# Attention and routed FFN layer: order of the first loads, and the turning and splitting of the first x by halves

## The reference

```python
k = x @ W_lat + b_lat                                # (2, 512, 128), keys and values of all heads
q = (x @ W_d + b_d).reshape(Bx, Tx, NH, L)           # 16 heads of 128
att = jnp.einsum('bhtl,bsl->bhts', q, k) * scale     # causal mask, softmax
y = jnp.einsum('bhts,bsl->bhtl', att, k)
return y @ W_proj + b_proj                           # then layer norm, FFN on 256 of 512 rows, layer norm
```

## Time and profile before

| what | before |
|---|---|
| time, median of 3 runs | 280.67 us (280.57 to 280.73) |
| the profiled execution's own time | 280.85 us |
| its span, first to last instruction | 279.1 us |
| TensorE busy | 271.7 us (97%) |
| VectorE, ScalarE, GpSimd busy | 218.8, 212.3, 154.2 us |

### The profile page before, as it was taken

How to read it: one execution, slowest core, us unless ns; L and a number is a source line. 1 busy time by engine, 2 the same in 40 slices (tenths; PEclk the granted TensorE clock), 3 DMA queues, 4 the chain that set the end, 5 groups by cost and what they waited for, 6 DMA issues and landing times.

```text
span 279.1 us, 6206 instructions
## 1 busy us (share of the span) xinstructions
PE 271.7 (97%) x1885; PEld 247.0 (89%) x1885; DVE 218.8 (78%) x701; ACT 212.3 (76%) x578; POOL 154.2 (55%) x214
## 2 busy tenths in 40 slices
PE   8999999999999999999999999999999999999991
PEld 4878999999999998999999999999999999999990
DVE  2698777777777777788789888899988887779882
ACT  3689877777787778887787877787777778879471
POOL 5458444444433336555666866665657847238652
PEclk9999999999999999999999999999999999999997
DMA  5594110111101111111111111110112200020151
GB/s 178 144 293 124 39 40 28 30 36 38 34 25 35 38 39 38 40 38 42 38 38 40 38 40 38 39 37 22 38 39 79 78 21 21 1 76 2 58 171 38
DMA packets 18842, 15.53 MB, mean 56 GB/s; under 512 B 1641, under 2 KB 18178, under 8 KB 18818
## 3 DMA queue, kind: packets, MB, share of 16 engines
q1 hardware_dynamic: 18242, 13.65, 16.4%
q0 software_dynamic: 576, 1.58, 1.6%
HBM read 12.60 MB, written 2.63 MB: 55 GB/s over the span
## 4 chain that ended last, share of the span: by engine, by line
PE 97%; DVE 0%; POOLq 0%; issue 0%; ACT 0%; DVEq 0%
PE bank L412 21%; PE bank L414 20%; PE bank L413 20%; PE bank L547 9%; PE ps_out L412 7%; PE ps_out L413 6%; PE ps_out L414 6%; PE bank L527 3%; PE bank L637 3%; PE bank L470 1%; PE bank L424 1%; POOLq L60 0%; PE bank L676 0%; PE bank L678 0%; PE bank L557 0%
## 5 line engine op out<-in xcount | busy, mean ns | idle before, releaser
L841 ACT ACTIVATE probs<-probs,negmax 128x512 f32<-128x512 f32 (+3 forms) x128 | 72.6, 575 | 6.0 <-DVE negmax L1026 4.6
L1384 POOL TENSOR_TENSOR wd_hi<-wd_raw,zero 128x256 fp32r<-128x256 f32 x31 | 23.8, 768 | 87.5 <-DVE probs L1098 84.5
L849 ACT CAST pT_hi<-bank 128x512 fp32r<-128x512 f32 (+2 forms) x96 | 43.4, 488 | 27.7 <-PE bank L547 27.3
L1026 DVE CUSTOM_DVE_ANT_0 probs<-bank,mask_row 128x512 f32<-128x512 f32 (+3 forms) x128 | 59.2, 482 | 0.7 <-PE bank L504 0.7
L1035 DVE TENSOR_TENSOR pT_lo<-bank,pT_hi 128x512 fp32r<-128x512 f32 (+2 forms) x96 | 52.8, 552 | 6.0 <-ACT pT_hi L849 5.6
L547 PEld LDWEIGHTS bank<-ident_r,prob_words 128*128 128x128 f32 x310 | 33.0, 140 | 5.5 <-ACT probs L893 0.4
L412 PE MATMUL ps_out<-wp_hi,yT_hi 128*128 128x256 f32 x124 | 37.0, 299 | 0.0
L412 PE MATMUL bank<-kT_hi,qT_hi 128*128 128x256 f32 (+2 forms) x94 | 36.5, 388 | 0.0
L413 PE MATMUL ps_out<-wp_lo,yT_hi 128*128 128x256 f32 x124 | 35.0, 282 | 0.0
L414 PE MATMUL ps_out<-wp_hi,yT_lo 128*128 128x256 f32 x124 | 34.9, 282 | 0.0
L1055 DVE TENSOR_TENSOR yT_lo<-bank,yT_hi 128x512 fp32r<-128x512 f32 x31 | 21.4, 690 | 15.9 <-PE bank L414 14.1
(11 more groups left out here) (203 smaller groups left out, 732.1 us busy)
## 6 DMA issues: line engine op xcount, KB each, us to landing
wd_raw<-in_L_attn_W_d SPq DMA_DIRECT2D x32, 128.0 KB, 2.2
wp_raw<-in_L_attn_W_proj SPq DMA_DIRECT2D x32, 128.0 KB, 2.1
wf_raw<-in_L_ffn_w SPq DMA_DIRECT2D x2, 1024.0 KB, 6.7
x_nat<-in_L_attn_x SPq DMA_DIRECT2D x4, 256.0 KB, 3.4
out<-z_all SPq DMA_DIRECT2D x4, 256.0 KB, 2.3
picked<-ranked SPq DMA_DIRECT2D x2, 258.0 KB, 2.7
wlat_raw<-in_L_attn_W_lat SPq DMA_DIRECT2D x1, 128.0 KB, 3.8
bproj_all<-in_L_attn_b_proj SPq DMA_DIRECT2D x1, 128.0 KB, 3.4
```

Of the source, the lines that this page charges most:

```text
L841: act.activation(p_tile(s, j), p_tile(s, j), ACT.Exp, bias=negmax[:, s, j:j + 1], scale=-1.0, accum_out=sums[:, s, j:j + 1]).then_inc(exp_ ...
L849: act.copy(pT_hi[:, dst], src).then_inc(pt_hi_done, 1)
L1026: dve.tensor_tensor_reduce(p_tile(s, j), score_bank[j], mask_row[:, (TILES - 1 - j) * P:], -SCALE, -MASKED, ALU.add, ALU.min, accum_out=ne ...
L1384: pool.tensor_tensor(hi, src, nothing, ALU.add).then_inc(hi_done, 1)
```

## The change

1. **Loads.** SyncE issues x half 0, W_lat, x half 1 in place of x half 0, x half 1, W_lat.
2. **Turning.** The first x is turned into four half banks: half 0 into `ps_t0[:, 0:256]` and `ps_t1[:, 0:256]`, half 1 into `ps_s2[:, 0:256]` and `ps_s10[:, 0:256]`. Every pair of transposes signals `x_turned` (four signals; before, two, both from the second half).
3. **Splitting.** ScalarE makes four copies of 128x256 in place of two of 128x512; VectorE four subtractions of 128x256 in place of two of 128x512. The counts of `x_turned`, `x_hi_done` and `x_split` for the second x move up by two.
4. **Idle matmuls.** One (512 columns) after the turning of half 0 (`BETWEEN`), and one after half 1 (`AWAKE`); before, two after half 1.
5. **The key projection.** The same six products in another order: hi·hi and lo·hi of c = 0, hi·hi and lo·hi of c = 1, hi·lo of c = 0, the bias, hi·lo of c = 1. The first one waits for three of four copies of x.
6. **The bias** is turned into `ps_s3`, since `ps_s2` now holds a half of x.

```diff
@@ -253,6 +253,11 @@
             _, _, src, dst = turns[n]
             return (ps_s3[:, P:3 * P] if n == 2 and at.fixed == UNITS else src), dst
+        x_banks = [[ps_t0[:, 0:KEEP], ps_t1[:, 0:KEEP]], [ps_s2[:, 0:KEEP], ps_s10[:, 0:KEEP]]]
+
+        def x_half(t, half, c):
+            return t[:, c, half * KEEP:(half + 1) * KEEP]
+
         def yT_of(at):
             return (last_yT_hi, last_yT_lo) if at.fixed == UNITS + 1 else (yT_hi, yT_lo)
@@ -295,7 +300,7 @@
                             body(Period(i * 2 + q, q, i))
                 p = first + 2 * times
-        WAKING, AWAKE = 6, 2
+        WAKING, BETWEEN, AWAKE = 6, (4,), (4,)
         CONSTS = 7
 
@@ -351,13 +356,14 @@
                 wait(sp, wp_split, unit - 1)
                 sp.dma_start(wp_raw[place][:], W_proj[bass.ds(head * LAT, LAT), :]).then_inc(wp_in[place], 16)
-            def load_x(b):
-                for j in range(0, TILES, 2):
+            def load_x(b, halves=range(2)):
+                for j in (half * 2 for half in halves):
                     sp.dma_start(x_nat[:, b * TILES + j:b * TILES + j + 2, :],
                                  x[b, j * P:(j + 2) * P].rearrange("(j p) d -> p j d", p=P)).then_inc(x_in[b][j // 2], 16)
-            load_x(0)
+            load_x(0, (0,))
             sp.dma_start(wlat_raw[:], W_lat.rearrange("(c p) l -> p c l", p=P)).then_inc(wlat_in, 16)
+            load_x(0, (1,))
             load_wd(0, 0, 0)
             sp.dma_start(bias_rows[0:HEADS, :], b_d.rearrange("(h l) -> h l", l=LAT)).then_inc(bias_in, 16)
             sp.dma_start(bias_rows[B_LAT:B_LAT + 1, :], b_lat.rearrange("(a l) -> a l", a=1)).then_inc(bias_in, 16)
@@ -417,39 +423,43 @@
                 for half in range(2):
                     pe.wait_ge(x_in[b][half], 16)
                     for c in range(CH):
-                        dst = (ps_t0, ps_t1)[c]
+                        dst = (ps_t0, ps_t1)[c][:, half * KEEP:(half + 1) * KEEP] if b else x_banks[half][c]
                         if b and half == 0:
                             pe.wait_ge(x_split, c + 1)
-                        for j in range(2 * half, 2 * half + 2):
+                        for j in range(2):
                             last = pe.transpose(dst[:, j * P:(j + 1) * P].bitcast(F32R),
-                                                x_words[:, b * TILES + j, c * P:(c + 1) * P], ident_r[:, :])
-                        if half:
+                                                x_words[:, b * TILES + 2 * half + j, c * P:(c + 1) * P], ident_r[:, :])
+                        if half or not b:
                             last.then_inc(x_turned, 1)
+                    if not b and half == 0:
+                        keep_awake(BETWEEN)
             def project_k_first():
                 w_hi, w_lo, x_hi, x_lo = wlat_hi, wlat_lo, xT_hi[0], xT_lo[0]
+                def term(w, x, c, first=False, last=False):
+                    return pe.matmul(ps_kT, w[:, c, :], x[:, c, :], start=first, stop=last, skip_group_check=True)
+
                 pe.wait_ge(wlat_hi_done, 1)
-                pe.wait_ge(x_hi_done, 1)
-                pe.matmul(ps_kT, w_hi[:, 0, :], x_hi[:, 0, :], start=True, stop=False, skip_group_check=True)
-                pe.wait_ge(x_hi_done, 2)
-                pe.matmul(ps_kT, w_hi[:, 1, :], x_hi[:, 1, :], start=False, stop=False, skip_group_check=True)
-                pe.wait_ge(x_split, 1)
-                pe.matmul(ps_kT, w_hi[:, 0, :], x_lo[:, 0, :], start=False, stop=False, skip_group_check=True)
+                pe.wait_ge(x_hi_done, 3)
+                term(w_hi, x_hi, 0, first=True)
                 pe.wait_ge(wlat_split, 1)
-                for c in range(CH):
-                    pe.matmul(ps_kT, w_lo[:, c, :], x_hi[:, c, :], start=False, stop=False, skip_group_check=True)
+                term(w_lo, x_hi, 0)
+                pe.wait_ge(x_hi_done, 4)
+                term(w_hi, x_hi, 1)
+                term(w_lo, x_hi, 1)
+                pe.wait_ge(x_split, 3)
+                term(w_hi, x_lo, 0)
                 pe.wait_ge(bias_in, 48)
-                pe.transpose(ps_s2[:, 0:BIASES], bias_rows[:, :], ident[0:BIASES, 0:BIASES]).then_inc(bias_turned, 1)
-                pe.wait_ge(x_split, CH)
-                pe.matmul(ps_kT, w_hi[:, 1, :], x_lo[:, 1, :], start=False, stop=True,
-                          skip_group_check=True).then_inc(kT_ready, 1)
+                pe.transpose(ps_s3[:, 0:BIASES], bias_rows[:, :], ident[0:BIASES, 0:BIASES]).then_inc(bias_turned, 1)
+                pe.wait_ge(x_split, 4)
+                term(w_hi, x_lo, 1, last=True).then_inc(kT_ready, 1)
             def project_k_second():
                 pe.wait_ge(kT_done, 1)
                 pe.wait_ge(kT_split, 1)
                 for c in range(CH):
-                    pe.wait_ge(x_split, CH + c + 1)
+                    pe.wait_ge(x_split, 2 * CH + c + 1)
                     last = product(ps_kT, (wlat_hi[:, c, :], wlat_lo[:, c, :]),
                                    (xT_hi[1][:, c, :], xT_lo[1][:, c, :]), c == 0, c == CH - 1)
                 last.then_inc(kT_ready, 1)
@@ -465,13 +475,13 @@
 
-            def keep_awake(times):
-                for _ in range(times):
-                    pe.matmul(ps_s3[:, :], still[:, :], still[:, :].unsqueeze(1).broadcast_to([P, TILES, P]),
+            def keep_awake(sizes):
+                for n in sizes:
+                    pe.matmul(ps_s3[:, 0:n * P], still[:, :], still[:, :].unsqueeze(1).broadcast_to([P, n, P]),
                               start=True, stop=True)
             pe.wait_ge(still_filled, 1)
-            keep_awake(WAKING)
+            keep_awake((TILES,) * WAKING)
 
             pe.wait_ge(ident_r_done, 1)
@@ -540,7 +550,7 @@
                     pe.wait_ge({AT_TURN: score_row_done, AT_RANK: rank_done}[at.fixed - 1][0], 1)
                 if at.fixed == 1 and n < CH:
-                    pe.wait_ge(x_split, CH + n + 1)
+                    pe.wait_ge(x_split, 2 * CH + n + 1)
                 a = 0
                 for i in tiles:
                     for j in range(i, TILES):
@@ -797,10 +807,16 @@
                 act.activation(qT_hi[place][:, P:], src[:, P:], ACT.Identity, bias=bias,
                                scale=1.0).then_inc(q_hi_done, 1)
-            def x_high(b):
+            def x_high_halves():
+                for half in range(2):
+                    for c in range(CH):
+                        act.wait_ge(x_turned, CH * half + c + 1)
+                        act.copy(x_half(xT_hi[0], half, c), x_banks[half][c]).then_inc(x_hi_done, 1)
+
+            def x_high_second():
                 for c in range(CH):
-                    act.wait_ge(x_turned, CH * b + c + 1)
-                    act.copy(xT_hi[b][:, c, :], (ps_t0, ps_t1)[c][:, :]).then_inc(x_hi_done, 1)
+                    act.wait_ge(x_turned, 2 * CH + c + 1)
+                    act.copy(xT_hi[1][:, c, :], (ps_t0, ps_t1)[c][:, :]).then_inc(x_hi_done, 1)
             def kT_high(b):
@@ -825,14 +841,14 @@
                 act.copy(k_last[b][:, :], ps_ks[b][:, SEQ - P:]).then_inc(k_last_done, 1)
                 act.copy(k_hi[b][:, :, :], ps_ks[b][:, 0:SEQ - P].rearrange("p (j l) -> p j l", l=LAT)).then_inc(k_hi_done, 1)
-            x_high(0)
+            x_high_halves()
             act.wait_ge(wd_in[0], 16)
             act.copy(wd_hi[0][:], wd_raw[0][:]).then_inc(wd_hi_done, 1)
             act.wait_ge(bias_done, 1)
             kT_high(0)
             split_queries(0, 0, 0, -1)
             kT_bias(0)
-            x_high(1)
+            x_high_second()
             def exps(at, js):
                 s = at.place(0)
@@ -987,10 +1003,15 @@
             dve.memset(still[:, :], 0.0).then_inc(still_filled, 1)
-            def x_low(b, c):
-                dve.wait_ge(x_hi_done, CH * b + c + 1)
-                dve.tensor_tensor(xT_lo[b][:, c, :], (ps_t0, ps_t1)[c][:, :],
-                                  xT_hi[b][:, c, :].bitcast(F32), ALU.subtract).then_inc(x_split, 1)
+            def x_low_half(half, c):
+                dve.wait_ge(x_hi_done, CH * half + c + 1)
+                dve.tensor_tensor(x_half(xT_lo[0], half, c), x_banks[half][c],
+                                  x_half(xT_hi[0], half, c).bitcast(F32), ALU.subtract).then_inc(x_split, 1)
+
+            def x_low_second(c):
+                dve.wait_ge(x_hi_done, 2 * CH + c + 1)
+                dve.tensor_tensor(xT_lo[1][:, c, :], (ps_t0, ps_t1)[c][:, :],
+                                  xT_hi[1][:, c, :].bitcast(F32), ALU.subtract).then_inc(x_split, 1)
             def kT_low(b):
                 dve.wait_ge(kT_hi_done, b + 1)
@@ -1008,10 +1029,12 @@
             dve.wait_ge(wlat_in, 16)
             dve.tensor_copy(wlat_hi[:], wlat_raw[:]).then_inc(wlat_hi_done, 1)
+            x_low_half(0, 0)
+            x_low_half(0, 1)
             for c in range(CH):
-                x_low(0, c)
+                x_low_half(1, c)
             dve.wait_ge(bias_turned, 1)
```

(6 more changed lines are left out.)

## The result

| what | before | after |
|---|---|---|
| time, median | 280.67 us (280.57 to 281.08, 7 runs) | 281.79 us (281.63 to 283.07, 7 runs) |
| the profiled execution's own time | 280.85 us | 281.79 us |
| its span | 279.1 us | 280.0 us |

What follows compares the result with a forecast made beforehand. TensorE's stream was taken to bound the kernel. A key-product loss of 0.14 to 0.34 us, beside 0.19 at the queries (the larger counts), gave 0.2 lost: 280.67 + 0.2 = 280.9 us, range 280.4 to 281.8.

Steps and rivals of the forecast that it cites:

- no change: Whole kernel: a loss of 0 to 0.5 us (62%), below the 0.56 us a measurement can tell; 75% with rivals.
- What bounds: Whole kernel: TensorE holds 97% of the chain, so a shift of its stream near the start moves the end as much.
- x half 1 is the new gate: Start: W_lat lands early and gates nothing; x half 1, issued 0.5 us later, lands between 4.9 and 6.1.
- L: Start: the time at which x half 1 lands, taken as 5.5 us, 3.7 us after its issue at 1.80.
- early landing: Start: x in 1 KB pieces lands sooner than W_lat in 512 B pieces, near 5.0, with no loss; not taken.
- From the landing on: Key products: copy from L + 0.53, first key load at L + 0.97 = 6.47, five products in 1.20 to 1.40 us.
- the bias as a gate: Fifth key product: the bias's weight load at 7.46 waits for its own transfers, expected again at about 7.4.
- the late clock: Start: a 0.6 us pause puts off TensorE's clock rise, 1.3 us more for six slow products, 282.2; 15%.
- third rival: Start: the clock rises earlier, or no key product waits; more than 0.56 us won, 280.0 or less; 5%.
- The term that I put at nothing: After 10 us: no difference expected; the smaller pieces' extra fixed parts on VectorE and ScalarE run beside TensorE's work.
- The queries' weights: Queries: `wd_hi` behind all x copies delays their load from 7.74 to 7.93, 0.19 us, beside the key products' loss.
- the cover at the bias: Before the bias product: 0.1 us or so by which its load came after the stream, expected to absorb loss.

Runs made afterwards that it cites:

- delay: The kernel before with four idle matmuls after the turning of the first x in place of two: 280.95 us, ratio 1.0011.

## Why the prediction was wrong, point by point

**The forecast was "no change", 0.2 us lost; measured were 1.0 us in the first group and 2.2 us in the second, the median being 1.1.** The direction of the likeliest time was right, its size a fifth. That the median lies in my range of 280.4 to 281.8, 0.01 us from its end, is luck: no term of the range stands for what took it there.

- *What bounds*: right. The whole of the start's shift (0.57 us) went through to the end, TensorE waits nowhere to take it up, and the same holds for 1.90 us in the kernel with the load order alone.
- *x half 1 is the new gate*: right; it stands in the chain with 3.90 us. The term L was mis-sized: I took 3.7 us from issue to landing, and it took 3.9 (4.0, 3.7, 3.8 in other runs), L = 5.70. I gave 3.9 as the longest of the x loads. What I weighed for an early landing (W_lat's small pieces are slow by themselves, x would be through sooner) may have a true half: with 1 KB pieces W_lat took 3.3 us in place of 3.5 to 3.8. But its pieces stand ahead of x now, and x was late. The term is 0.2 us too small.
- *From the landing on*: right to 0.03 us. The first key product's load came at L + 0.94 (expected 0.97), ScalarE's copy at L + 0.45 (0.53, at the slow clock), the five products took 1.26 from the first load (1.20 to 1.40). At L = 5.7 the text has 0.5, and the measured shift is 0.57.
- **The step that failed first: the bias as a gate.** I read the late weight load at 7.46 as a wait for a transfer, promised a cover for part of the loss, and a stop for any gain. But the row that I showed has `<-issue` and not a transfer, and the semaphore `bias_in` had its last landing at 6.23 us in that trace, 1.2 us ahead of the load. The load comes 0.33 us after the start of the fifth product in both traces (7.13 and 7.46; 7.67 and 8.00), 0.31 to 0.33 us after it in every profile at the fast pace, and 0.55 us after it in the two with the late clock (8.78 and 9.33). The row of the run with two instructions on ScalarE:

```profile
7.26 0.14 PEld L443 LDWEIGHTS bank<-ident,bias_rows 25*128 25x128 f32 x1 [0.35 <-issue]
```

  It is bound to the end of the product ahead, and not to its data. Whether the 25 rows or the plain f32 keep this load from going ahead like the others, no run tells. So there was no gate to hide a loss behind. My sum let the bias product follow the fifth product's stream at once. It follows 0.17 us later, before (7.36 and 7.53) and after (7.90 and 8.07).
- **The step that failed most, in the second group: the late clock, given 15%.** I priced it at 1.3 us for six slow products and called the pause "little". It happened in three of seven and three of six runs of the changed kernel, and in six of ten of the one with W_lat in 1 KB pieces. The measured price is 1.4 us at the queries (1.98 against 0.57). The mechanism, the place and nearly the price were in the text; the chance had no row behind it. The trace before couldn't tell it, since it has no pause. The run without idle matmuls shows what two of them are worth there: up to 2.1 us.
- *The clock in the first group* rose earlier than before, by 5.75 in place of some 6.2. That is my third rival's mechanism. It gave back some 0.15 us or more: from the first load to the end of the fifth product's stream 1.26 us went by (6.64 to 7.90) in place of 1.40 (5.96 to 7.36). So the late load by itself costs more than 0.57.
- **The term that I put at nothing**: 0.36 us after 30 us, 0.21 of it the step that two instructions more on ScalarE make at the loop's entry, the rest open. I wrote that a difference after 10 us would be wrong by my account, and that the smaller pieces cost nothing. Without the step the first group would be near 281.4 to 281.5, by the run with four more instructions.
- *The queries' weights*: the same size as the key chain, expected; `wd_lo` came 0.36 us ahead of its use, so it was the smaller, as the rule "the larger counts" allows.

The first group in a sum, from the 0.2 of my sum on: 0.17 for the cover at the bias that isn't there, 0.17 for half 1's later landing (first key product's load at 6.64 in place of 6.47), and 0.03 by the end of the queries make 0.57. With the 0.36 after 30 us that is 0.93, against 0.94 between the two profiled executions.

No version beats the kernel before. The best of the changed ones by its ratio (1.0016), without the pause and without the step at the loop's entry, is at 281.44 us. What is left there is 0.53 us at the start, with half 1's late landing, and 0.16 us after 30 us.

## What to carry to other kernels

A transfer moved up is paid by the one behind it: before swapping loads, ask which of the two has the longer chain behind it, here x with transposes, copies and five products against W_lat with one copy. Idle matmuls ahead of TensorE's first real work aren't waste, and a wait that leaves TensorE without them for half a microsecond, before its clock has risen, can cost far more than the wait, in some executions only; so look at every run's time and not at the profile alone. Before calling a late weight load a wait for a transfer, look at what its row names and when the transfer landed. When a shift grows in a part that nobody touched, look for an engine that enters a loop late, and try a few instructions more or less on it.

## What the runs showed of the hardware

- The clock's rise moves from one execution to the next, and a pause ahead of it can put it off. In the six profiles without a pause (before, delay, two copies on ScalarE, 1 KB pieces in the kernel before, and the two with the pause filled) it came between 5.8 and 6.4 us by the pace. Without the idle matmuls it came at 3.9 us and with the old load order at 4.9, ahead of their pauses, and with W_lat on ScalarE's queue near 4.4, just behind a pause of 0.48 us. In the changed kernel's first group it came within the pause of 0.71 us, and near 9.6 us in the two profiles of long executions, behind pauses of 0.88 us (changed kernel) and 1.14 us (load order alone). A pause of 0.43 us by its profile, with W_lat in 1 KB pieces, went with six long runs of ten. The granted clock is given as 1.00 from 1 to 10 us in both groups; the pace of equal matmuls and weight loads shows the rise.
- Position of code on ScalarE: two instructions more cost 0.21 us per execution at the loop's entry, one or four more nothing, with 0.38 to 0.40 or 0.07 to 0.12 us of idle time there.
- A weight load of 25x128 in f32 starts only after the product ahead has streamed (0.31 to 0.33 us after its start at the fast pace, 0.55 at the slow), while 128x128 loads go ahead under it.
- Transposes that read a block with a stride of two columns: 1.04 us for eight in place of 0.64.
- A 256 KB transfer lands 0.6 to 1.0 us later when a 128 KB one in 512 B pieces is issued ahead of it (3.7 to 4.0 against 3.0 to 3.1), on another engine's queue as well.
